# A Mamba scan on one core: the step sizes' last addition moves to TensorE and ScalarE, and GpSimd weighs one more unit of states

## The reference

```python
def _mamba(x, inproj, conv_w, conv_b, xproj, dt_w, dt_b, Alog, Dp, outproj):
    u, z = jnp.split(x @ inproj, 2, axis=-1)              # 512 channels each
    uc = silu(conv(u))                                    # 4 taps
    dt, Bm, Cm = jnp.split(uc @ xproj, [16, 32], axis=-1) # 16 states
    delta = jax.nn.softplus(dt @ dt_w + dt_b)             # the step sizes
    A = -jnp.exp(Alog)
    def step(h, inp):
        u_t, d_t, B_t, C_t = inp
        dA = jnp.exp(d_t[..., None] * A)
        h = dA * h + (d_t * u_t)[..., None] * B_t[:, None, :]
        y_t = jnp.einsum('bdn,bn->bd', h, C_t)
        return (h, y_t)
    ...
    y = (ys + uc * Dp) * silu(z)
    return y @ outproj
```

## Time and profile before

| | |
|---|---|
| three runs | 1573.46, 1573.46, 1575.78 us; median 1573.46 us |
| profiled execution | 1577.74 us, its span 1575.50 us |
| scan phase, first scan to the end of the last period | 247.46 to 1090.70 us |
| busy share of the span: PE, DVE, ACT, POOL | 75%, 74%, 49%, 58% |
| mean granted TensorE clock | 0.86 of full |

### The profile page before, as it was taken

How to read it: one execution, slowest core, us unless ns; L and a number is a source line. 1 busy time by engine, 2 the same in 40 slices (tenths; PEclk the granted TensorE clock), 3 DMA queues, 4 the chain that set the end, 5 groups by cost and what they waited for, 6 DMA issues and landing times. The chain is left out here.

```text
span 1575.5 us, 14568 instructions
## 1 busy us (share of the span) xinstructions
PE 1188.5 (75%) x4900; PEld 663.6 (42%) x4900; DVE 1168.5 (74%) x1029; ACT 766.0 (49%) x1018; POOL 917.2 (58%) x410
## 2 busy tenths in 40 slices
PE   6899982897659887288883763445663999999998
PEld 4788820232113332033221210111232778787887
DVE  4433356999999999999999999995277654544544
ACT  5333364677555675457755554441134543333440
POOL 4420017999999999999999999983355000000000
PEclk9999995898769998698987766666885999999999
DMA  5133016442365232633233343210502230301102
GB/s 188 47 114 107 27 59 280 147 160 69 147 214 187 76 130 105 253 140 114 108 135 125 153 152 133 88 45 14 208 27 64 97 134 1 134 0 54 66 27 79
DMA packets 44415, 173.73 MB, mean 110 GB/s; under 512 B 5681, under 2 KB 10289, under 8 KB 31554
## 3 DMA queue, kind: packets, MB, share of 16 engines
q1 hardware_dynamic: 44354, 172.98, 29.8%
HBM read 138.89 MB, written 34.08 MB: 110 GB/s over the span
## 5 line engine op out<-in xcount | busy, mean ns | idle before, releaser
L1057 POOL TENSOR_TENSOR scan_dbu<-scan_rep,scan_bc 128x1024 f32<-128x1024 f32 x256 | 597.3, 2364 | 43.2 <-DMA scan_rep<-dd_rows 36.6
L996 ACT ACTIVATE scan_hs<-scan_rep,scan_neg_a 128x1024 f32<-128x1024 f32 x256 | 285.4, 1118 | 347.4 <-DVE scan_hc L1115 305.8
L1105 DVE TENSOR_TENSOR_SCAN scan_hs<-scan_hs,scan_dbu 128x1024 f32<-128x1024 f32 x192 | 439.0, 2286 | 11.3 <-ACT scan_hs L996 10.9
L904 PE MATMUL scan_ysum<-scan_hc,scan_sel 128*32 128x512 f32 x1024 | 176.3, 821 | 236.0 <-DVE scan_hc L1115 235.9
L1115 DVE TENSOR_TENSOR scan_hc<-scan_hs,scan_bc 128x1024 f32<-128x1024 f32 x192 | 234.9, 1223 | 6.1
L904 PEld LDWEIGHTS scan_ysum<-scan_hc,scan_sel 128*32 128x32 f32 x1024 | 36.3, 132 | 356.2 <-issue 356.2
L829 PE MATMUL scan_pb<-scan_xin,scan_inwf 128*128 128x512 f32 x384 | 172.8, 604 | 0.0
L1063 POOL TENSOR_TENSOR scan_hc<-scan_hc,scan_bc 128x1024 f32<-128x1024 f32 x64 | 151.1, 2361 | 12.9 <-DVE scan_hc L1105 12.6
L1105 DVE TENSOR_TENSOR_SCAN scan_hc<-scan_hs,scan_dbu 128x1024 f32<-128x1024 f32 x64 | 145.8, 2278 | 11.2 <-POOL scan_dbu L1057 11.2
L829 PEld LDWEIGHTS scan_pb<-scan_xin,scan_inwf 128*128 128x128 f32 x384 | 72.4, 193 | 103.3 <-issue 103.3
L32 PE MATMUL ffn_sl<-ffn_tanh_s,xm_s 128*128 128x512 f32 x384 | 106.0, 411 | 2.3 <-DVE ffn_tanh_s L1814 2.3
(11 more groups left out here) (186 smaller groups left out, 1626.6 us busy)
## 6 DMA issues: line engine op xcount, KB each, us to landing
scan_rep<-dd_rows SPq DMA_DIRECT2D x64, 1024.0 KB, 5.6
scan_bc<-bc_rows SPq DMA_DIRECT2D x32, 512.0 KB, 5.9
dd_rows<-scan_dd SPq DMA_DIRECT2D x16, 1024.0 KB, 3.8
ffn_wt<-in_ew SPq DMA_DIRECT2D x16, 1024.0 KB, 7.8
scan_inwf<-fold SPq DMA_DIRECT2D x12, 512.0 KB, 3.8
cond<-scan_bc SPq DMA_DIRECT2D x16, 256.0 KB, 3.2
scan_xin<-cond SPq DMA_DIRECT2D x4, 1024.0 KB, 7.5
y_all<-scan_yo SPq DMA_DIRECT2D x8, 512.0 KB, 3.1
```

The lines of the kernel that those rows point to most:

```text
L904: mm = nc.tensor.matmul(ysum[i * D32:(i + 1) * D32, h, :], sel[:], hc[:, (s0 + i) % HCR, h * CT:(h + 1) * CT], start=False, stop=last, til ...
L996: nc.scalar.activation(hs[:, s % HSR, :], rep[:, e % REPS, 0, :], ACT.Exp, scale=neg_a[:, k % 2, NI * dc + i, r // NI:r // NI + 1]).then_i ...
L1057: nc.gpsimd.tensor_tensor(dbu[:, s % DBR, :], rep[:, e % REPS, 1, :], bc[:, j, 0, :], ALU.mult).then_inc(dbu_done, 1)
L1105: nc.vector.tensor_tensor_scan(states, hs[:, s % HSR, :], dbu[:, s % DBR, :], 0.0, ALU.mult, ALU.add).then_inc(scan_done, 1)
```

## The change

Periods 0, 3, 7, 11 and 15 (`late_step`) keep their way; the other eleven are the **changed periods**. In a changed period `w`, for the step sizes of period `w + 1`:

- GpSimd no longer adds. TensorE does it, as two identity matmuls for each half of the columns into a `pb` bank (`step_total`, key "a"), ahead of its other chores and of group 1, that is behind group 0; they wait for Ln. ScalarE copies each half back over `dd[:, 0]`, at r = 6 (`TOTAL_AT`), behind that unit's `decay`.
- GpSimd's `step_du` moves from r = 7 to r = 10 and waits for the copies instead of the add.
- GpSimd weighs five units, 0, 3, 9, 11 and 13, in place of 0, 4, 8 and 12; VectorE weighs one fewer.

In periods 0, 3, 7, 11 and 15 GpSimd weighs 0, 3, 10 and 13.

```diff
+POOL_UNITS, LATE_POOL_UNITS = (0, 3, 9, 11, 13), (0, 3, 10, 13)
+
+def late_step(w):
+    return w == 0 or w % DC == DC - 1
...
 def pool_unit(s):
     r = s % UPP
-    return r % NI == 0
+    return r in (LATE_POOL_UNITS if late_step(s // UPP) else POOL_UNITS)
...
+    total = [("a", k, p + 1, h) for h in range(HALVES)] if r == 1 and not late_step(DC * k + p) else []
...
-    return (old.get((p, r), []) if done else []) + (new.get((p, r), []) if more else []) + step
+    return total + (old.get((p, r), []) if done else []) + (new.get((p, r), []) if more else []) + step
...
-POOL_STEP_AT, LATE_POOL_STEP_AT = (6, 7), (8, 9)
+TOTAL_AT = 6
+POOL_STEP_AT, LATE_POOL_STEP_AT = (None, 10), (8, 9)
...
+        def wait_delta(eng, w):
+            if w == 0 or late_step(w - 1):
+                eng.wait_ge(delta_done, own_adds(w))
+            else:
+                freed(eng, *(("a", *divmod(w, DC), h) for h in range(HALVES)))
...
         def step_du(engine, eng, w):
             k, dc = divmod(w, DC)
-            eng.wait_ge(delta_done, w + 1)
+            wait_delta(eng, w)
...
+            def step_total(k, dc, h):                      # TensorE
+                out, done = claim(("a", k, dc, h))
+                pe.wait_ge(soft, (HALVES + 2) * (DC * k + dc + 1))
+                freed(pe, *(("t", k, dc, i) for i in range(HALVES)))
+                for i in range(2):
+                    mm = nc.tensor.matmul(out, ident[:], dd[:, i, h * CT:(h + 1) * CT], start=(i == 0), stop=(i == 1))
+                mm.then_inc(done, 1)
...
+            def step_total(k, dc, h):                      # ScalarE
+                x, free = ready(act, "a", k, dc, h)
+                nc.scalar.activation(dd[:, 0, h * CT:(h + 1) * CT], x, ACT.Copy).then_inc(free, 1)
...
+                    if r == TOTAL_AT and not late_step(w):
+                        for h in range(HALVES):
+                            step_total(k, p + 1, h)
```

More of the change, by code:

```diff
@@ L496, with own_adds @@
 POOL_LAG = 3
+POOL_UNITS, LATE_POOL_UNITS = (0, 3, 9, 11, 13), (0, 3, 10, 13)
+def late_step(w):
+    return w == 0 or w % DC == DC - 1
+def own_adds(w):
+    return sum(v == 0 or late_step(v - 1) for v in range(w + 1))
 def pool_unit(s):
     r = s % UPP
-    return r % NI == 0
+    return r in (LATE_POOL_UNITS if late_step(s // UPP) else POOL_UNITS)
 POOL_BEFORE = [0, *itertools.accumulate(int(pool_unit(s)) for s in range(UNITS_ALL))]
@@ L721, in store_step @@
             def store_step(w):
-                sp.wait_ge(delta_done, w + 1)
+                wait_delta(sp, w)
                 sp.wait_ge(du_done, w + 1)
@@ L908, in add_states @@
                             mm.then_inc(ysum_done, 1)
-            does = {"u": in_proj, "x": x_proj, "t": step_size, "z": z_gate, "o": out_proj, "skip": skip}
+            does = {"u": in_proj, "x": x_proj, "t": step_size, "z": z_gate, "o": out_proj, "skip": skip, "a": step_total}
             pe.wait_ge(vecs, 6 * 16)
@@ L1021, in _ @@
                 k, p = divmod(w, DC)
-                step_in_at, exp_at, ln_at = LATE_STEP_AT if p + 1 == DC or w == 0 else STEP_AT
+                step_in_at, exp_at, ln_at = LATE_STEP_AT if late_step(w) else STEP_AT
                 for r in range(UPP):
@@ L1074, in _ @@
             for w in range(PERIODS):
-                add_at, du_at = LATE_POOL_STEP_AT if w % DC == DC - 1 or w == 0 else POOL_STEP_AT
+                add_at, du_at = LATE_POOL_STEP_AT if late_step(w) else POOL_STEP_AT
                 for r in range(UPP):
```

## The result

The changed kernel is slower: median 1600.54 us of four runs (1598.40 to 1604.05), against 1574.62 for the kernel before in the same job. The ratio is 1.0153, with a 95% interval of 1.0120 to 1.0185, so 19 to 29 us. The forecast was +8.8 us, to 1582.3, with a range up to 1600; the ratio on the base of the forecast, 1573.46, gives 1597.5. The direction and the mechanism held; the size was 2.7 times what I had summed. The time lies in the upper end of the stated range and outside the likeliest rival's own range of 1577 to 1592: the range reached that far only because it made room for the half-clock rival.

A forecast was written before the change was run, and what follows sets the result against it. VectorE sets the pace, with GpSimd 0.86 us to spare in a period. Terms: +3.8 (chain), −2.6 (k = 3), +6.6 (clock), +1.0 (B and C rows) = +8.8 us on 1573.46, so 1582.3 us; range 1566 to 1600.

The forecast's parts named there:

- the likeliest rival: Whole kernel: TensorE's chain late, with drops of the clock; 1582.3 us, own range 1577 to 1592, chance 0.50.
- the half-clock rival: Group 0 and the new matmuls in the eight changed k = 0 to 2 periods run at 1.2 GHz; 1617 us, chance 0.12.
- VectorE's and GpSimd's paces: Each changed period: VectorE 50.47 us with one product fewer, GpSimd 50.87 us for its 22 operations.
- The ceiling of −15.1 us: Eleven changed periods at GpSimd's pace without a new wait: 559.6 against 574.7 us, a gain of 15.1.
- The chain behind the new work: TensorE behind group 0, eight changed periods of k = 0 to 2: late input projections delay silus and VectorE; +3.8 us.
- 1 us of cover: Decay of unit 7: ready at 479.8, scan due at 480.8, at full clock; at half clock the cover is gone.
- B and C rows: Group 2 waits for GpSimd's unit 11 in period 2, delaying the B and C projection; +1.0 us for three times, bounds 0 and 3.
- The clock: Drops after TensorE's idle time before group 0, in four of eight periods, no longer absorbed: 4 x 1.6 = +6.6 us.
- k = 3: Three changed periods without input projection hold GpSimd's pace: 152.6 against 155.19 us, −2.6 us.
- its half case: Half clock through group 0 and the new matmuls in only half of the eight periods: some 1600 us.
- I take it as ready: GpSimd assumed ready to weigh unit 3 when its scan ends, so group 0 starts 1.15 us later.
- The step sizes' later load: SyncE's store and load behind the later step_du: five us or more left before the first piece is needed, so nothing.

The follow-up runs named there:

- The fastest run: Against the kernel before: softplus computed directly as ln(1 + exp(x)), no addition, GpSimd's products at units 0, 4, 6, 8, 12 in all periods; 1557.8 us.
- e5_not_last: The changed kernel with GpSimd's products at units 0, 4, 6, 8, 12 (0, 4, 8, 12 in the other periods); 1580.7 us.
- the kernel without an addition: Direct softplus, five GpSimd products in every period: 1557.8 us at units 0, 4, 6, 8, 12; 1572.9 us at the change's 0, 3, 9, 11, 13.

## Why the prediction was right, and where it was off

**VectorE's and GpSimd's paces** were right: 50.47 and 50.87 forecast, 50.45 and 50.9 measured in the run above. The ceiling of −15.1 us for eleven periods was not passed by any run that kept the addition. The fastest run, with five products in all sixteen periods, gained 17; sixteen times the same 1.37 us would be 22 (an estimate from the forecast's own terms).

**The chain behind the new work** was right as a mechanism, step for step: GpSimd releases group 0 at 14.95 us, the matmuls take 3.5, the silu waits for the input projection, the scan comes 3.15 later. The stalls were forecast at units 9, 12 and 14, and are there. There is another at unit 7, for which I had counted 1 us of cover at full clock and none at half: it stands in exactly the eight periods in which group 0 ran at the lower clock, 0.25 to 3.15 us long, and in period 1 it is the longest stall of all. What failed is the slack that the sum took for granted elsewhere. It leaves some 0.7 us in period 4 without the new matmuls (2.5 and 0.6, less 1.15 and 1.26), and in the run without an addition that period has no stall behind the one at unit 5. But in that run units 12 and 14 of periods 1, 5, 8 and 9 stall for 6.1 us in sum, and unit 1 of six periods for 7.4 us, where the sum has only its 1.0 for the B and C rows. Together they are nearly all of the gain that did not come.

**The clock was mis-sized.** "Four of the eight periods show it now … The other four go from about 1 to about 2.2 us of idle … I leave them at nothing." The working has a slip as well: 14.00 − 12.43 is 1.57, and four times that is 6.3, not 6.6. Group 0 ran at the lower clock, in whole or part, in six of the eight periods and in two of the three of k = 3, and in periods 1, 8, 9 and 14 the drop reached into the new matmuls. What it costs can be read against period 2, where both run at full clock; from group 0 to the row behind the new matmuls is 5.39 us there:

```profile
377.20 1.92 PE L932 MATMUL scan_ysum<-scan_hc,scan_sel 128*32 128x512 f32 x16 [0.88 <-POOL scan_hc L1098]
...
382.59 10.47 PE L849 MATMUL scan_pb<-scan_xin,scan_inwf 128*128 128x512 f32 x24
```

The eight periods take 53.9 us for it in sum, and eight times 5.39 is 43.1: the lower clock cost 10.8 us where the sum had 6.6. With the 2.1 us by which group 0 came late in period 1 (below) this is 6.3 us more than forecast, and the eight periods took 16.6 in place of 10.4: the gap is accounted for. The rows of period 14, in windows of TensorE alone (busy, granted clock), from behind its gate:

```profile
1018.00:1020.00 2.00, 0.00 (x0) 0.78 0.00 0
1020.00:1022.00 2.00, 0.55 (x4) 0.50 0.00 0
1022.00:1024.00 2.00, 2.00 (x13) 0.50 0.00 0
1024.00:1026.00 2.00, 2.00 (x10) 0.52 0.00 0
1026.00:1028.00 2.00, 2.00 (x6) 1.00 0.00 0
```

The pause itself was mis-sized too: in seven of the eleven changed periods TensorE's gate ran at full clock and ended 11.1 to 11.2 us into the period, where period 4 had 12.8 before, so that the pause was 3.9 us and more. My "about 2.2" had kept the old ends. The length of the pause alone doesn't tell what follows: behind 2.29 us in period 9 the group took 2.94 us, behind 3.00 in period 13 it took 1.92. The Trainium skill, TensorE: Matmul & The Clock Gate, Part 1, has the lower clock as the default, released by activity. The trace agrees with its direction: behind the pause of period 14 the clock reads 0.50, and with zeros in the pause it reads 1.00 from 475 to 485 us. The rival that took the rule to its end (1617 us) was too dark, the sum too bright; its half case, "some 1600", is nearest to what was measured.

**"I take it as ready" was wrong in three periods.** In periods 1, 13 and 14 GpSimd had no lead left. Here in period 14 (VectorE ended the scan of unit 3 at about 1017.0):

```profile
1012.02 6.98 POOL L1092 TENSOR_TENSOR scan_dbu<-scan_rep,scan_bc 128x1024 f32<-128x1024 f32 x3
1018.95 2.35 POOL L1098 TENSOR_TENSOR scan_hc<-scan_hc,scan_bc 128x1024 f32<-128x1024 f32 x1
```

GpSimd is busy with `dbu` until 1018.95 and the product comes 1.9 us late. Where VectorE isn't stalled, GpSimd is the slower engine, and the same balance that should bring the gain makes its products late. Period 13 still ran at VectorE's pace (50.45 us); in period 14 the late group and the lower clock made the copies late, and VectorE waited 2.97 us at unit 7. With 1.4 us of waits in period 12, k = 3 gave +0.9 in place of −2.6.

**The B and C rows** were forecast at +1.0, and the five other periods together lost 3.3; 2.3 of that are waits at unit 1 of periods 3, 7 and 11 (0.65 to 0.93 us), where the kernel before has none. The run without an addition, with the same places, has them too (1.2 to 1.8), and so has the run with unit 4 in place of 3 (1.2 to 1.5). In e5_not_last, without place 11, there are none. The remaining 1.0 us is not traced.

**The step sizes' later load** cost nothing, as forecast: GpSimd waited for the replicated pieces only at the very start of the phase, beside two waits under 1 us.

What stays open: what the change would take with the clock held up and group 0 left where it is, since no run holds the clock without also moving group 0. Nor is it shown which of the places 3 and 11 costs the 12 us in the kernel without an addition.

## What to carry to other kernels

Work moved onto an engine off the path still has a place in that engine's order: read what stands behind it and when each is due, not the engine's share of busy time. When a slow engine takes over part of a group that another waits for, look first at its last member, above all where late work stands behind the group: here that one choice was worth 22 us in group 0, more than the rebalancing itself, and next to nothing in group 2 of the same kernel. And before moving an operation to a third engine, look for a form that doesn't need it.

## What the runs showed of the hardware that was not expected

- Two engines can each run at its own pace for several periods when one has a lead of up to four units: VectorE at 50.45 us beside GpSimd at 50.9 in the fastest run. A balance read over a few periods can flatter both.
- Matmuls whose weights are all zero kept the granted clock at 1.00 where they filled the pause (475 to 485 us in period 4), and all eleven groups behind them took 1.92 us.
- A switch of ScalarE's activation table costs 1.28 us here, and the next activation starts 1.30 us after the load does (498.09 to 499.39). The Trainium skill, ScalarE: Activation LUTs, "What ACT_TABLE_LOAD costs", has a drain of about that length on top, 2.66 us in all; the trace shows none, and in the changed kernel the load runs before the wait for TensorE is over (509.15 against 513.30 above), so its cost is hidden in such a wait.
